# V in blocks of two tiles by seven half-size products instead of eight, spread over three slots, in a gated cross-attention and feed-forward kernel

## The chip, the cores and the metric

The kernel runs on one core of a Trainium2 chip. The metric is the device time of one execution in microseconds (us), the median of the runs shown. Five engines work beside each other, each through its own instructions in order: PE (TensorE, matrix products), ACT (ScalarE), DVE (VectorE), POOL (GpSimd) and SP (SyncE, which issues most of the DMAs). They wait for each other through semaphores.

## The reference

x is 8 batches of 1024 rows of 512 numbers; the context has the same shape.

```python
# cross-attention, causal, one head of 512
q, k, v = layernorm(x) @ w_q, ctx @ w_k, ctx @ w_v
attn = softmax(where(causal, q @ k.T / sqrt(512), -inf))
x = x + tanh(g_xattn) * (attn @ v)
# feed-forward, width 2048; w1 and w2 rounded to -1, 0, 1 by the mean of their absolute values
h = gelu(layernorm(x) @ ternary(W1).T + b1)
x = x + tanh(g_ffn) * (h @ ternary(W2).T + b2)
```

## The kernel before

Every number that enters a product is split into two fp16 parts, an upper one (the rounded value) and a lower one (the rest); ACT makes the upper part, DVE the lower. A product is then three passes: upper by upper, lower by upper, upper by lower (`PASSES`).

The rows of x are 64 tiles of 128, 8 tiles to a batch. The attention part goes in 64 slots, one for each tile t; below, n is t modulo 8, the tile's place in its batch. In a slot PE does, in this order (`slot`, L1304): the scores of tile t against its first n+1 context tiles (L1319, 12 matmuls for each 512 columns or part of them); the query product of tile t+2 (`t_product`, L1281, 24 matmuls of 256 columns); V of context tile t+1 (`v_product`, L1300, 12 matmuls of 512 columns); and attn times V of tile t-1 (here PV, L1349, 3(n) matmuls of 512 columns, 24 where n is 0). Scores need nothing of PV, so PV of one tile runs while the softmax of the next goes on.

DVE's slot (L897 to L986) runs in program order, so a late instruction makes all behind it late: add the causal mask (L909), the row maximum (L911) and the exponent's bias (L915); the statistics of the layer norm of tile t+5; the lower part of the softmax weights (L929); of the query product (L873); the normalised rows (L850); a ternary step for a chunk of weights in some slots (L1091, L1093); the lower part of V (L880); the output row (L956, L959, L963, after PV); and, in some slots, the maximum of the next batch's context (L821) or the lower part of that context (L756). ACT's slot follows the same chain: exponential (L573), upper part of the weights (L578), of the query product (L588), of the rows (L596), of V (L601), of the next context (L563). POOL makes the reciprocal root (L446) and the lower part of the rows (L450).

Near the end, the first rows of the feed-forward part are prepared: normalised by DVE from `FIRST_Y` on, summed by POOL into the blocks that seven half-size products need (`y_sums`), split (`y_upper` on ACT, `y_lower` on POOL), turned by a DMA on SP (`turn_y`, L334), and used by PE's first unit (`unit_first`, L1203), which runs in slot 63. DVE adds and subtracts blocks of the first weight matrix (`weight_sums`, L1004). The feed-forward part then runs 64 units, each with seven half-size products and 32 matmuls of 512 columns; the change moves a few steps into its first three.

Of the kernel before, what the change touches and what calls it, by code (L numbers as in the profile page):

```python
# [18 lines left out]
def gated_block(nc, x, ctxT, g_xattn, g_ffn, wqT, wkT, wv, w1T, b1c, w2T, b2, out):  # L19
    B, _, DC, S = ctxT.shape  # L20
# [26 lines left out]
    with es:  # L47
# [47 lines left out]
        cmax = sb("cmax", [P, 2])  # L95
# [16 lines left out]
        x2_in = raw[:, :].rearrange("p (t d) -> p t d", d=D)  # L112
# [17 lines left out]
        wS = [half for t in (a_s, wv_s)  # L130
# [10 lines left out]
        a_ps = y_ps = [s_ps[:, 0:D], s_ps[:, D:2 * D], e_ps[:, 0:D], e_ps[:, D:2 * D]]  # L141
        bank_a, bank_b, bank_c = [v_ps[:, :], o_ps[:, :]], m_ps[:, :], t_ps[:, :, :].rearrange("p a n -> p (a n)")
# [3 lines left out]
        ctx_in = sem("ctx_in")  # L146
        ctx_in0 = [sem(f"ctx_in0_{h}") for h in range(2)]
# [15 lines left out]
        turn_issued, turn_free = sem("turn_issued"), sem("turn_free")  # L163
        t_mm, t_hi, t_split = sem("t_mm"), sem("t_hi"), sem("t_split")
# [7 lines left out]
        w_loaded = [sem(f"w_loaded{i}") for i in range(WR)]  # L172
        w_summed, w_total, w_total_all, w_thresh = sem("w_summed"), sem("w_total"), sem("w_total_all"), sem("w_thresh")
# [12 lines left out]
        y_stored = [sem(f"y_stored{i}") for i in range(4)]  # L186
# [5 lines left out]
        def col(c, n=1):  # L192
# [7 lines left out]
        TOTALS = m_ps[:, 3 * P:3 * P + 2]  # L200
# [18 lines left out]

# [12 lines left out]

        PV0 = 2
# [13 lines left out]
        FIRST_Y = NT - 7  # L247
# [1182 lines left out]
```

## Time and profile before

| | |
|---|---|
| median of 3 runs (lowest, highest) | 1590.83 us (1590.52, 1591.98) |
| the profiled execution's own time | 1590.56 us |
| its span in the profile | 1588.7 us |
| matmuls, all passes | 10024 |
| granted TensorE clock, mean of the span | 0.997 of full speed |
| chain that ended last, by engine | PE 95%, DVE 3%, DMA 1%, issue 1% |

The span is what the profiler's records cover; 1.9 us of the execution lie around it. The attention part takes the first 756 us of the span, the feed-forward part the rest. One batch of eight slots takes 88.6 us on PE. The profile models the ends of matmuls, so the pace of PE is read from the starts of successive groups. In the timelines a row's start is when the instruction began on its engine, and two rows of one engine without a wait between them overlap by somewhat under 0.1 us.

### The profile page before, as it was taken

The page shows a single profiled execution, that of the slowest core. Times are in us where ns is not written, and L with a number is a line of the kernel's source. Part 1 is how long each engine was busy: PE and PEld are TensorE (multiplying, and loading weights), DVE is VectorE, ACT ScalarE, POOL GpSimd, SP SyncE. Part 2 cuts the span into 40 slices and gives each one's busy share as a digit, 9 for nine tenths or more (in the row PEclk, how much of TensorE's full clock was granted, in tenths as well). Part 3 has the DMA queues.
Part 4 walks back from the last instruction along what each step waited for, and adds up shares of the span by engine and source line. Part 5 has one row for each costly group of instructions (what it writes and reads, how often), then busy time and mean ns, then how long its engine had stood idle before and what let it go on. Part 6 is the DMA issues. An engine that isn't in the chain of part 4 may idle for free.

```text
span 1588.7 us, 26066 instructions
## 1 busy us (share of the span) xinstructions
PE 1567.5 (99%) x10024; PEld 979.6 (62%) x10024; DVE 1094.7 (69%) x1824; ACT 811.6 (51%) x1448; POOL 481.6 (30%) x468
## 2 busy tenths in 40 slices
PE   7899999999999999999999999999999999999998
PEld 4556555565656565564666666666666666666665
DVE  7766656577787777766567667766776676767654
ACT  2334444433332333333666666666666666666654
POOL 4311111111111111134144444444433453345330
PEclk9999999999999999999999999999999999999999
DMA  8547667654656655553322242233332332324110
GB/s 212 130 103 192 149 182 153 175 137 121 165 128 163 141 160 145 129 123 78 81 77 77 47 100 77 77 67 80 81 87 68 66 98 79 77 47 100 51 51 27
DMA packets 307964, 170.81 MB, mean 108 GB/s; under 512 B 268208, under 2 KB 268224, under 8 KB 306688
## 3 DMA queue, kind: packets, MB, share of 16 engines
q1 hardware_dynamic: 306368, 166.52, 43.0%
q10 hardware_dynamic: 1296, 2.36, 0.4%
q8 instruction: 79, 1.29, 0.3%
q14 instruction: 45, 0.37, 0.1%
q0 software_dynamic: 176, 0.27, 0.1%
HBM read 70.53 MB, written 33.55 MB: 66 GB/s over the span
## 4 chain that ended last, share of the span: by engine, by line
PE 95%; DVE 3%; DMA 1%; issue 1%; ACT 0%; SPq 0%; DVEq 0%
PE s_ps L1254 14%; PE e_ps L1254 14%; PE s_ps L1319 11%; PE o_ps L1349 11%; PE v_ps L1300 10%; PE t_ps L1281 10%; PE t_ps L1198 7%; PE o_ps L1198 7%; PE v_ps L1198 7%; PE m_ps L1198 3%; DMA ctx_s<-in_wqT 1%; DMA raw<-in_ctxT 0%; DVE cmax L821 0%; DVE wv_s L1004 0%; PE e_ps L1349 0%
## 5 line engine op out<-in xcount | busy, mean ns | idle before, releaser
L1056 DVE SCALAR_TENSOR_TENSOR v_s<-xnT,sc,v_s 128x512 f16<-128x512 f32 x256 | 239.0, 954 | 106.3 <-ACT v_s L681 106.3
L674 ACT ACTIVATE xnT<-tT,b_s 128x256 f32<-128x256 f32 x384 | 174.0, 500 | 182.9 <-DVE tT L1050 66.6
L1254 PE MATMUL s_ps<-w_s,v_s 128*128 128x512 f16 x1024 | 262.8, 379 | 0.0
L1254 PE MATMUL e_ps<-w_s,v_s 128*128 128x512 f16 x1024 | 262.8, 379 | 0.0
L573 ACT ACTIVATE p<-s_ps,ebias,esc 128x128 f32<-128x128 f32 (+3 forms) x64 | 53.2, 831 | 339.3 <-DVE ebias L915 339.3
L1319 PE MATMUL s_ps<-ctx_s,tT 128*128 128x512 f16 (+3 forms) x1152 | 197.7, 326 | 3.2 <-DVE tT L873 3.2
L1349 PE MATMUL o_ps<-v_s,pT 128*128 128x512 f16 x840 | 191.6, 379 | 0.1
L681 ACT ACTIVATE v_s<-xnT,sc 128x512 f16<-128x512 f32 x256 | 176.3, 712 | 7.5
L1300 PE MATMUL v_ps<-wv_s,ctx_s 128*128 128x512 f16 x768 | 176.5, 379 | 1.2 <-DVE v_s L880 0.8
L1254 PEld LDWEIGHTS e_ps<-w_s,v_s 128*128 128x128 f16 x1024 | 100.2, 98 | 120.8
L1281 PE MATMUL t_ps<-xnT,a_s 128*128 128x256 f16 x1488 | 172.7, 273 | 0.5 <-ACT a_s L649 0.5
L1319 PEld LDWEIGHTS s_ps<-ctx_s,tT 128*128 128x128 f16 x1152 | 105.8, 98 | 95.1 <-DVE tT L873 4.1
L1281 PEld LDWEIGHTS t_ps<-xnT,a_s 128*128 128x128 f16 x1488 | 144.8, 98 | 22.8 <-issue 0.9
L501 POOL TENSOR_TENSOR tT<-tT 128x512 f32<-128x512 f32 x64 | 81.5, 1273 | 245.7 <-ACT tT L701 245.7
L446 POOL TENSOR_TENSOR rstd<-var_s,minus_half 128x1 f32<-128x1 f32 x61 | 34.0, 557 | 382.8 <-DVE var_s L844 382.8
L1349 PEld LDWEIGHTS o_ps<-v_s,pT 128*128 128x128 f16 x840 | 82.1, 98 | 97.2 <-DMA pT<-p_s 0.6
L1254 PEld LDWEIGHTS s_ps<-w_s,v_s 128*128 128x128 f16 x1024 | 100.2, 98 | 67.1
L1300 PEld LDWEIGHTS v_ps<-wv_s,ctx_s 128*128 128x128 f16 x768 | 74.9, 98 | 78.9 <-issue 1.0
L450 POOL TENSOR_TENSOR xn_both<-xn_both 128x512 f16<-128x512 f32 x61 | 70.9, 1162 | 165.0 <-ACT xn_both L596 165.0
L1038 DVE COPY tT<-t_ps 128x512 f32<-128x512 f32 x64 | 44.3, 692 | 92.8 <-PE t_ps L1198 92.8
L471 POOL TENSOR_TENSOR rstd<-var_s,minus_half 128x1 f32<-128x1 f32 x64 | 35.1, 548 | 226.9 <-DVE var_s L1016 226.9
L880 DVE SCALAR_TENSOR_TENSOR v_s<-v_ps,v_s 128x512 f16<-128x512 f32 x64 | 44.1, 689 | 74.9 <-ACT v_s L601 74.9
(176 smaller groups left out, 2411.9 us busy)
## 6 DMA issues: line engine op xcount, KB each, us to landing
out_y<-x_ring SPq DMA_DIRECT2D x128, 256.0 KB, 2.2
x_ring<-in_x SPq DMA_DIRECT2D x63, 256.0 KB, 2.9
raw<-in_ctxT SPq DMA_DIRECT2D x7, 2048.0 KB, 7.9
raw<-out_y SPq DMA_DIRECT2D x44, 256.0 KB, 3.7
w_in<-in_w1T SPq DMA_DIRECT2D x16, 512.0 KB, 3.9
w_in<-in_w2T SPq DMA_DIRECT2D x16, 512.0 KB, 3.9
x_ring<-out_y SPq DMA_DIRECT2D x20, 256.0 KB, 3.5
xnT<-xn_both SPq DMA_TRANSPOSE x128, 2.7
```

What stands on the lines that cost most here:

```text
L450: g.tensor_tensor(xn_s[:, r, LO], xn32[:, r], xn_s[:, r, HI], ALU.subtract).then_inc(xn_lo, 1)
L501: g.tensor_tensor(rr[:, R3], rr[:, R3], rr[:, R5], ALU.add).then_inc(c22_sum, 1)
L573: a.activation(p32[:, 0:w], s_ps[:, 0:w], ACT.Exp, bias=ebias[:, r:r + 1], scale=esc[:, (s // TB) % 2:(s // TB) % 2 + 1], accum_out=rowsum ...
L674: a.activation(g32n[:, j, half * 2 * P:(half + 1) * 2 * P], src, ACT.Gelu, bias=b1_s[:, f:f + 1], scale=1.0 / YN).then_inc(g_act, 1)
L681: a.activation(g_s[:, U % 2, j, HI], g32n[:, j], ACT.Copy, scale=col(C_SG)).then_inc(g_hi, 1)
L1056: v.scalar_tensor_tensor(out=g_s[:, U % 2, j, LO], in0=g32n[:, j], scalar=col(C_SG), in1=g_s[:, U % 2, j, HI], op0=ALU.mult, op1=ALU.subtr ...
L1198: last_mm = mm(bank[:, p * 2 * P:(p + 1) * 2 * P], w, yT[g % 2][:, a, row, c, :], start=(first and p == 0 and a == HI and c == 0), stop=(a ...
L1254: last_mm = mm(y_ps[i], g_s[:, U % 2, j, a, i * P:(i + 1) * P], w2_s[:, f, :], start=(U % UG == 0 and n == 0 and a == HI), stop=(U % UG == ...
L1281: last_mm = mm(bank[:, dd], a_s[:, aa, c, d * P:(d + 1) * P], xnT[:, pr, xa, c, :], start=(n == 0 and c == 0), stop=(n == 2 and c == DC - 1))
L1300: last_mm = mm(v_ps[:, :], ctx_s[:, par, ca, c, j * P:(j + 1) * P], wv_s[:, va, c, :], start=(n == 0 and c == 0), stop=(n == 2 and c == DC ...
L1319: last_mm = mm(s_ps[:, lo:hi], tT[:, pr, ta, c, q * P:(q + 1) * P], ctx_s[:, par, ca, c, lo:hi], start=(n == 0 and c == 0), stop=(n == 2 a ...
L1349: last_mm = mm(o_bank(last, s), pT[:, (s - 1) % 2, pa, j], v_s[:, par, va, j], start=(n == 0 and j == 0), stop=(n == 2 and j == jn))
```

## The change

V of the first eight context tiles is made as before. The other 56 tiles are taken as 28 pairs of neighbouring tiles (u = 0 to 27). A pair's V is a 256 x 512 result from a 256 x 512 context block and the 512 x 512 weights; cut in halves each way it would be eight products of half size, and is made here by seven, of 6 matmuls of 256 columns each (three passes, two chunks). For this POOL makes four sums and differences of the context's blocks for each pair (`ctx_parts`), ACT and DVE split them (`ctx_parts_upper`, `ctx_parts_lower`), and the same is done once for the weights (slots 3 to 5). Products 1, 6, 5 and 3 add up in one PSUM region, and between them ACT copies the state out (`v_first`, `v_second`, `v_third`); product 2 has a region of its own, 7 and 4 share one. DVE adds three results (`v11`, `v22`, `v21`) and, with ACT, splits the four blocks of V (`v12_...`, `vd_...`, `v21_...`).

A pair's steps are spread over four slots: in slot 4+2u the context's sums and its split; in slot 5+2u products 1 and 2; in slot 6+2u product 6 right behind the scores, 5 and 7 behind the query product, 3 behind PV; in slot 7+2u product 4. So in a slot with even t PE does products 6, 5, 7, 3, and in one with odd t products 4, 1, 2 (4 of the pair before). Scales are lowered so that the sums fit into fp16.

With it go other moves. The context comes in quarters, each loaded, and its maximum taken, by itself in odd slots. The ternary step takes three instructions, in other slots, and its last three chunks move into the feed-forward part's first units. The feed-forward's second weight matrix lies where the context was loaded, and the rows of the first two groups are loaded one by one, a slot later (`FIRST_Y`); `weight_sums` come a slot earlier; the third `y_upper` and `y_lower` move into unit 0.

```diff
...
+        SPLIT_AT, PRE_AT, MAIN_AT, LAST_AT = 4, 5, 6, 7
...
+        def pair(t, at):
+            u, odd = divmod(t - at, 2)
+            return u if not odd and 0 <= u < NP else None
...
+        for b in range(2, B):
+            for q, at in enumerate((-3, -1, 1, 3)):
+                MAX_AT[TB * (b - 1) + at] = (b, (q,))
...
-                  **{b * TB + n: "T" for b in range(3, 7) for n in (4, 5, 6, 8)}}
+                  **{t: "T" for t in (29, 30, 31, 37, 38, 39, 45, 46, 53, 54, 55, 56, 60)}}
...
-        FIRST_Y = NT - 7
+        FIRST_Y = NT - 6
...
+            def ctx_parts(u):
...
+                pool.wait_ge(ctx_in[q], ctx_landed(b, q))
+                pool.wait_ge(sums_split, u)
+                g.tensor_tensor(sums32[:, 0], a21, a22, ALU.add).then_inc(sums_made, 1)
+                g.tensor_tensor(sums32[:, 2], a11, a21, ALU.subtract).then_inc(sums_made, 1)
+                pool.wait_ge(sums_made, 4 * u + 1)
+                g.tensor_tensor(sums32[:, 1], sums32[:, 0], a11, ALU.subtract).then_inc(sums_made, 1)
+                pool.wait_ge(sums_made, 4 * u + 3)
+                g.tensor_tensor(sums32[:, 3], a12, sums32[:, 1], ALU.subtract).then_inc(sums_made, 1)
...
+            def ctx_parts_upper(u):
+                act.wait_ge(sums_made, 4 * u + 4)
...
+            def v_third(u):
+                act.wait_ge(vp_mm[5], u + 1)
+                a.activation(vr[:, 1], vp_a, ACT.Copy).then_inc(vr_out, 1)
+            def v12_upper(u):
+                _, q, par = pair_at(u)
+                act.wait_ge(vp_mm[3], u + 1)
+                a.activation(v_s[:, par, HI, 2 * q, D // 2:D], vp_a, ACT.Copy, scale=V_DOWN).then_inc(vb_hi, 1)
...
+                if pre is not None:
+                    ctx_parts_upper(pre)
+                if main is not None:
+                    v_second(main)
                 if not last or t < NT:
                     softmax(it, s)
                 if not last or t < NT - T_LEAD:
...
+                if t + 1 < TB:
                     v_upper(it, s)
+                if main is not None:
+                    v_third(main)
+                if pre is not None:
+                    v_first(pre)
+                if tail is not None:
+                    v21_upper(tail)
+                if main is not None:
+                    v12_upper(main)
+                    vd_upper(main)
+                if split is not None:
+                    b, q, par = pair_at(split)
+                    ctx_upper(b, par, q)
...
+            def v22(u):
+                dve.wait_ge(vp_mm[7], u + 1)
+                dve.wait_ge(vr_out, nth_of(u, 3))
+                v.tensor_tensor(vr[:, 1], vr[:, 1], vp_c, ALU.add).then_inc(vb_sum, 1)
...
+            def v12_lower(u):
+                _, q, par = pair_at(u)
+                dve.wait_ge(vb_hi, nth_of(u, B12_DONE))
...
-                for m, n in terns[:1]:
-                    ternary(m, n)
-                if not last or t + 1 < NT:
+                if pre is not None:
+                    ctx_parts_lower(pre)
+                if tail is not None:
+                    v21(tail)
+                if pre is not None:
+                    v11(pre)
+                if tail is not None:
+                    v21_lower(tail)
+                if main is not None:
+                    v22(main)
...
+                if t + 1 < TB:
                     v_lower(it, s)
...
-                if last and t == NT - 2:
+                if last and t == NT - 3:
                     weight_sums(0)
                     weight_sums(1)
-                if last and t == NT - 1:
+                if last and t == NT - 2:
                     weight_sums(2)
                     weight_sums(3)
...
+                if main is not None:
+                    v12_lower(main)
+                    vd_lower(main)
+                if t == 1:
+                    ctx_lower(0, 0, 3)
+                if t in MAX_AT:
+                    batch, quarters = MAX_AT[t]
+                    for q in quarters:
+                        ins = ctx_quarter(batch, q)
...
+                if split is not None:
+                    b, q, par = pair_at(split)
+                    ctx_lower(b, par, q)
...
+                v.tensor_scalar(w_neg[:, :], src, col(nth), None, ALU.is_lt).then_inc(w_negs, 1)
+                v.tensor_scalar(w_dst(n), src, col(th), None, ALU.is_gt).then_inc(w_negs, 1)
+                dve.wait_ge(w_negs, 2 * n + 2)
+                v.tensor_tensor(w_dst(n), w_dst(n), w_neg[:, :], ALU.subtract).then_inc(w_ternary, 1)
...
+                left, right, bank, first = {
+                    1: (block(0, 0), weight(0, 0), vp_a, True),
+                    6: (part(1), weight_part(1), vp_a, False),
+                    5: (part(0), weight_part(0), vp_a, False),
+                    3: (part(3), weight(1, 1), vp_a, False),
+                    2: (block(0, 1), weight(1, 0), vp_b if u else vp_b0, True),
+                    7: (part(2), weight_part(2), vp_c, True),
+                    4: (block(1, 1), weight_part(3), vp_c, False)}[k]
+                for n, (ca, va) in enumerate(PASSES):
+                    for c in range(2):
+                        last_mm = mm(bank, left(ca, c), right(va, c), start=(first and n == 0 and c == 0),
+                                     stop=(n == 2 and c == 1), skip_group_check=True)
+                last_mm.then_inc(vp_mm[k], 1)
...
+            def v_six(u):
+                pe.wait_ge(vr_out, nth_of(u, 1))
+                pe.wait_ge(sums_split, u + 1)
...
+            def v_three(u):
+                pe.wait_ge(vr_out, nth_of(u, 3))
+                v_part(u, 3)
...
+                if main is not None:
+                    v_six(main)
                 if s > 0 and (not last or t < NT - T_LEAD):
                     t_product(it, s)
...
+                if main is not None:
+                    v_five(main)
+                    v_seven(main)
+                if tail is not None:
+                    v_four(tail)
+                if pre is not None:
+                    v_pre(pre)
...
-                if not last or t + 1 < NT:
+                if t + 1 < TB:
                     v_product(it, s)
...
                     last_mm.then_inc(pv_mm, 1)
+                if main is not None:
+                    v_three(main)
...
```

PE, slots 33 and 34 (n = 1 and 2) before: s_ps are the scores, t_ps the query product, v_ps V, o_ps PV.

```order
L1319 MATMUL s_ps<-ctx_s,tT 128x256 x12
L1281 MATMUL t_ps<-xnT,a_s 128x256 x24
L1300 MATMUL v_ps<-wv_s,ctx_s 128x512 x12
L1349 MATMUL o_ps<-v_s,pT 128x512 x3
L1319 MATMUL s_ps<-ctx_s,tT 128x384 x12
L1281 MATMUL t_ps<-xnT,a_s 128x256 x24
L1300 MATMUL v_ps<-wv_s,ctx_s 128x512 x12
L1349 MATMUL o_ps<-v_s,pT 128x512 x6
```

The same two slots in the changed kernel, where e_ps and v_ps at L1568 are the products:

```order
L1667 MATMUL s_ps<-ctx_s,tT 128x256 x12
L1628 MATMUL t_ps<-xnT,a_s 128x256 x24
L1568 MATMUL e_ps<-v_work,ctx_s 128x256 x6
L1568 MATMUL e_ps<-wv_s,ctx_s 128x256 x6
L1568 MATMUL v_ps<-wv_s,ctx_s 128x256 x6
L1713 MATMUL o_ps<-v_s,pT 128x512 x3
L1667 MATMUL s_ps<-ctx_s,tT 128x384 x12
L1568 MATMUL e_ps<-v_work 128x256 x6
L1628 MATMUL t_ps<-xnT,a_s 128x256 x24
L1568 MATMUL e_ps<-v_work 128x256 x12
L1713 MATMUL o_ps<-v_s,pT 128x512 x6
L1568 MATMUL e_ps<-wv_s,v_work 128x256 x6
```

In slot 33 products 4, 1 and 2 stand where V stood; in slot 34 product 6 has moved ahead of the query product, 5 and 7 stand where V stood, and 3 has come behind PV.

DVE, from the end of slot 32 (n = 0) into slot 33 before: L963 is the output row, L909 the next slot's mask.

```order
L880 SCALAR_TENSOR_TENSOR v_s<-v_ps,v_s 128x512
L956 RECIPROCAL rinv<-rowsum 128x1
L959 TENSOR_SCALAR osc<-rinv,fsc 128x1
L963 SCALAR_TENSOR_TENSOR x_ring<-o_ps,osc,x_ring 128x512
L909 TENSOR_TENSOR s_ps<-s_ps,causal 128x128
```

The same place in the changed kernel (L1047 is `v22`, L1059 `v12_lower`, L1067 `vd_lower`, L946 the lower part of the next context, L1164 the mask):

```order
L1047 TENSOR_TENSOR vr<-vr,e_ps 128x256
L1221 RECIPROCAL rinv<-rowsum 128x1
L1224 TENSOR_SCALAR osc<-rinv,fsc 128x1
L1228 SCALAR_TENSOR_TENSOR x_ring<-o_ps,osc,x_ring 128x512
L1059 SCALAR_TENSOR_TENSOR v_s<-e_ps,v_s 128x256
L1067 SCALAR_TENSOR_TENSOR v_s<-vr,v_s 128x2x256
L946 SCALAR_TENSOR_TENSOR ctx_s<-raw,csc,ctx_s 128x4x256
L1164 TENSOR_TENSOR s_ps<-s_ps,causal 128x128
```

Three instructions have come between the output row and the next slot's mask, where there was none; the first of them needs product 3 of the slot.

DVE, the second half of slot 33 before, up to the mask of slot 34 (L850 the normalised rows, L821 half of the context's maximum):

```order
L850 TENSOR_SCALAR xn_both<-x_ring,mv,rstd 128x512
L880 SCALAR_TENSOR_TENSOR v_s<-v_ps,v_s 128x512
L956 RECIPROCAL rinv<-rowsum 128x1
L959 TENSOR_SCALAR osc<-rinv,fsc 128x1
L963 SCALAR_TENSOR_TENSOR x_ring<-o_ps,osc,x_ring 128x512
L821 TENSOR_REDUCE cmax<-raw 128x1
L909 TENSOR_TENSOR s_ps<-s_ps,causal 128x128
```

And in the changed kernel (L1032 is `ctx_parts_lower`, L1053 `v21`, L1041 `v11`, L1075 `v21_lower`, L1017 a quarter of the maximum):

```order
L1104 TENSOR_SCALAR xn_both<-x_ring,mv,rstd 128x512
L1032 SCALAR_TENSOR_TENSOR v_work<-v_work,csc 128x1024
L1053 TENSOR_TENSOR vr<-vr,e_ps 128x256
L1041 TENSOR_TENSOR vr<-vr,v_ps 128x256
L1075 SCALAR_TENSOR_TENSOR v_s<-vr,v_s 128x256
L1221 RECIPROCAL rinv<-rowsum 128x1
L1224 TENSOR_SCALAR osc<-rinv,fsc 128x1
L1228 SCALAR_TENSOR_TENSOR x_ring<-o_ps,osc,x_ring 128x512
L1017 TENSOR_REDUCE cmax<-raw 128x1
L1164 TENSOR_TENSOR s_ps<-s_ps,causal 128x128
```

One instruction for V has become four, and the maximum is half as long.

## Rows read from the trace of the kernel before

**Rows 1.** which engine is busy, from the page (busy us, share, instructions)
```profile
PE 1567.5 (99%) x10024; PEld 979.6 (62%) x10024; DVE 1094.7 (69%) x1824; ACT 811.6 (51%) x1448; POOL 481.6 (30%) x468
```

**Rows 2.** PE's waits over the whole run (total us, times, longest us)
```profile
PE t_ps L1198 <- DVE wv_s L1004: 3.9, 1, 3.9
```

**Rows 3.** the timeline of PE, slots 25 and 26 (start us, length us, instructions)
```profile
311.32 5.34 PE L1349 MATMUL o_ps<-v_s,pT 128*128 128x512 f16 x24
316.50 1.47 PE L1319 MATMUL s_ps<-ctx_s,tT 128*128 128x256 f16 x12
317.81 2.78 PE L1281 MATMUL t_ps<-xnT,a_s 128*128 128x256 f16 x24
320.43 2.75 PE L1300 MATMUL v_ps<-wv_s,ctx_s 128*128 128x512 f16 x12
323.02 0.81 PE L1349 MATMUL o_ps<-v_s,pT 128*128 128x512 f16 x3
```

**Rows 4.** the timeline of DVE in the same slots
```profile
318.01 0.30 DVE L909 TENSOR_TENSOR s_ps<-s_ps,causal 128x128 f32<-128x128 f32 x1 [0.48 <-PE s_ps L1319]
...
320.19 0.43 DVE L929 SCALAR_TENSOR_TENSOR p_s<-p,p_s 128x256 f16<-128x256 f32 x1 [0.16 <-ACT p_s L578]
...
324.45 0.15 DVE L956 RECIPROCAL rinv<-rowsum 128x1 f32<-128x1 f32 x1
...
325.56 2.28 DVE L821 TENSOR_REDUCE cmax<-raw 128x1 f32<-128x2048 f32 x1
...
327.82 0.29 DVE L909 TENSOR_TENSOR s_ps<-s_ps,causal 128x128 f32<-128x128 f32 x1
...
330.34 0.56 DVE L929 SCALAR_TENSOR_TENSOR p_s<-p,p_s 128x384 f16<-128x384 f32 x1 [0.38 <-ACT p_s L578]
330.82 0.69 DVE L873 SCALAR_TENSOR_TENSOR tT<-t_ps,tT 128x512 f16<-128x512 f32 x1
331.43 0.54 DVE L850 TENSOR_SCALAR xn_both<-x_ring,mv,rstd 128x512 f32<-128x512 f32 x1
```

**Rows 5.** the timeline of ACT in the same slots
```profile
323.22 0.60 ACT L601 ACTIVATE v_s<-v_ps 128x512 f16<-128x512 f32 x1 [0.15 <-PE v_ps L1300]
...
332.54 0.58 ACT L601 ACTIVATE v_s<-v_ps 128x512 f16<-128x512 f32 x1
```

**Rows 6.** instructions by line and form (busy us, mean ns | idle before)
```profile
L756 DVE SCALAR_TENSOR_TENSOR ctx_s<-raw,csc,ctx_s 128x1024 f16<-128x1024 f32 x32 | 40.3, 1277 | 0.0
...
L563 ACT ACTIVATE ctx_s<-raw,csc 128x1024 f16<-128x1024 f32 x32 | 35.5, 1133 | 4.0 <-DVE csc L836 4.0
...
L641 ACT ACTIVATE v_s<-v_s 128x1792 f16<-128x1792 f32 x17 | 28.8, 1696 | 27.7 <-POOL v_s L482 27.7
...
L478 POOL TENSOR_TENSOR v_s<-v_s 128x256 f32<-128x256 f32 x17 | 12.3, 721 | 0.0
...
L1091 DVE TENSOR_SCALAR g<-w_in,sc 128x1024 f16<-128x1024 f32 x16 | 12.0, 748 | 0.1
...
L929 DVE SCALAR_TENSOR_TENSOR p_s<-p,p_s 128x256 f16<-128x256 f32 x8 | 3.4, 424 | 1.0 <-ACT p_s L578 1.0
L578 ACT ACTIVATE p_s<-p 128x256 f16<-128x256 f32 x8 | 3.3, 416 | 0.3
...
L1004 DVE TENSOR_TENSOR a_s<-a_s,w_s 128x1024 f16<-128x1024 f16 x2 | 1.3, 684 | 0.0
```

**Rows 7.** DVE while Pool works, a threshold instruction in slot 36
```profile
440.09 2.28 DVE L1093 SCALAR_TENSOR_TENSOR w_s<-w_in,sc,g 128x1024 f16<-128x1024 f32 x1
```

**Rows 8.** the timeline of POOL at the same time
```profile
440.13 1.16 POOL L450 TENSOR_TENSOR xn_both<-xn_both 128x512 f16<-128x512 f32 x1 [2.80 <-ACT xn_both L596]
```

**Rows 9.** the SP queue near the end of the attention part
```profile
722.68 4.24 SPq L334 DMA_TRANSPOSE ctx_s<-v_s  x1
```

**Rows 10.** the timeline of POOL just before that
```profile
719.07 3.59 POOL L488 TENSOR_TENSOR v_s<-v_s 128x1792 f16<-128x1792 f32 x1 [4.29 <-ACT v_s L641]
```

**Rows 11.** PE where the feed-forward part begins
```profile
736.04 1.04 PE L1198 MATMUL v_ps<-ctx_s,w_s 128*128 128x256 f16 x8
```

More of the change, by code:

```diff
@@ L19, in gated_block @@
 def gated_block(nc, x, ctxT, g_xattn, g_ffn, wqT, wkT, wv, w1T, b1c, w2T, b2, out):
-    B, _, DC, S = ctxT.shape
+    B, _, NQ, DC, QS = ctxT.shape
+    S = NQ * QS
     N, D = x.shape
@@ L129, in gated_block @@
         w1v = w1_s[:, :].rearrange("p (d c) (m b n) -> p d c m b n", d=2, c=2, m=FC // 2, b=2)
-        wS = [half for t in (a_s, wv_s)
+        wS = [half for t in (wv_s, a_s)
               for half in (t[:, 0].rearrange("p c d -> p (c d)"), t[:, 1].rearrange("p c d -> p (c d)"))]
@@ L185, in gated_block @@
         y_mm, y_done = sem("y_mm"), sem("y_done")
-        y_stored = [sem(f"y_stored{i}") for i in range(4)]
+        y_stored, X2_ALL = x2_stored[0:4], 16 * (NT // 8 + 1)
         (C_TANH0, C_TANH1, C_G0, C_G1, C_WMAX, C_BMAX, C_MA, C_PA, C_PW, C_PG, C_SA, C_SW, C_SG,
@@ L369, in slot @@
                 if t == 1:
-                    load_ctx(1)
-                if s % TB == 7 and (not last or t + 9 < NT):
-                    load_ctx(it * 2 + s // TB + 2)
+                    for q in range(NQ):
+                        load_ctx(1, q)
             for i in range(8):
                 sp.sem_inc(x2_stored[i], 16)
-            for i in range(4):
-                sp.sem_inc(y_stored[i], 16)
             for r in range(2):
@@ L460, in slot @@
                         y_sums(e // 2)
[L461 removed]
+                if last and e in (2, 4):
                     y_lower(e // 2 - 1)
@@ L538, in _ @@
                     last_sum(U + 1)
+                if U == 0:
+                    y_lower(2)
                 if U in ROWS_Q0:
@@ L723, in _ @@
                     unit_copy(U + 1)
+                if U == 0:
+                    y_upper(2)
                 if U - 1 in ROWS_Q0:
@@ L900, in slot @@
                 i, r = s % TB, s % 2
+                split, pre, main, tail = pair(t, SPLIT_AT), pair(t, PRE_AT), pair(t, MAIN_AT), pair(t, LAST_AT)
                 terns = w_turn(t, "T")
@@ L1247, in back @@
                 pe.wait_ge(g_split, 4 * U + n + 1)
+                if U < UG and n == 0:
+                    pe.wait_ge(w_ternary, NW // 2 + 2 * U + 2)
                 for i in range(GT):
@@ L1306, in slot @@
                 i = s % TB
+                pre, main, tail = pair(t, PRE_AT), pair(t, MAIN_AT), pair(t, LAST_AT)
                 if not last or t < NT:
```

348 lines of the change are left out of this document (262 added, 86 removed).

## The prediction

> **What bounds the kernel now.** I read the busy shares first, then PE's waits, then the timelines of slots 25 and 26 (n = 1 and 2, where slots are shortest). PE is busy for 99% of the span and DVE for 69% [rows 1]; the largest wait of PE outside the start is one of 3.9 us [rows 2]. So PE's work is the time, and work taken from PE is time saved, as long as PE is not made to wait. The reader should see in the timelines how little protects that. DVE is late already: the scores of slot 26 follow PV at 323.02 + 0.65, take 1.95 and so end near 325.6, but the mask comes at 327.82, behind the context's maximum [rows 3, 4]. That costs nothing before, since PE uses a slot's softmax only in the next slot.
>
> **PE's work.** 24 matmuls of 512 columns take 316.50 - 311.32 = 5.18 us, 24 of 256 take 320.43 - 317.81 = 2.62, V of one tile 323.02 - 320.43 = 2.59 [rows 3]. A pair cost 5.18; seven products are 42 matmuls of 256, 42 x 2.62/24 = 4.585. The difference of 0.595 by 28 pairs is **-16.7 us**. Accumulating into a region read in between changes nothing in this pace; each such read is a wait, taken below.
>
> A rule speaks against this. The Trainium skill (TensorE: Matmul & The Clock Gate, section Back-to-back issue gap) gives a sustained spacing of about 131 ns for 512 columns and 81 ns for 128; an estimate between them is 98 ns for 256, and by it a pair would rise from 3.1 to 4.1 us, +27 us in all. The rows show 216 and 109 ns in this kernel; the measurement decides.
>
> **The new wait, n = 2.** Product 3 of an even slot waits for `v_third`, which ACT reaches only behind softmax, query product and normalised rows of the same slot, and these hang on DVE. PE now needs DVE's slot within the slot. I follow it from E, the end of product 3 in the slot n = 0.
> - ACT starts 0.20 after PE's end (323.02 to 323.22) [rows 3, 5]. `v12_upper` 0.42, `vd_upper` 0.60, the context's upper part 1.13, then its lower part on DVE 1.28 [rows 5, 6]; less some 0.25 of overlap, DVE is free for the mask of n = 1 at E + 3.4. The scores are there at E + 1.5 (316.50 to 318.01) [rows 3, 4]: 1.9 late.
> - Slot n = 1 on DVE: mask to softmax's lower part 2.18, to the query product's 0.48, to the normalised rows 0.61 [rows 4], these 0.46; `ctx_parts_lower` 1.20 (as the context's, 1.28 less overlap) [rows 6]; `v21`, ACT's `v21_upper` and gaps 0.91; `v21_lower` 0.36 (all three 256 wide, 0.42 each) [rows 6], held 0.3 by POOL (below); reciprocal to maximum 1.11, a quarter maximum half of 2.28, 1.14 [rows 4]. Sum 8.75: mask of n = 2 at E + 12.15.
> - Slot n = 2: 2.52 + 0.48 + 0.61 [rows 4], to ACT's instruction behind the rows 1.11 (331.43 to 332.54) [rows 4, 5], `v_third` 0.42, start of PE 0.1: product 3 can start at E + 17.4.
> - PE is there at: slot 1, 1.31 + 2.62 + 18 x 0.109 + 0.65 = 6.54; slot 2, 1.95 + 0.65 + 2.62 + 1.31 + 1.29 = 7.82; E + 14.4. **Wait 3.0 us.**
>
> No row shows a 256-wide sum from PSUM: 128 wide is 0.30, 512 wide 0.69 [rows 4], so the five 256-wide links give -0.65 to +1.35; I take 0.42, from rows of that width. The wait is then 2.1 (without POOL) to 4.4. It comes in slots 10, 18, 26, 34, 42 and 50: **+18.0**. In slot 58 no maximum stands before it (-1.14), but statistics of a feed-forward row do (+0.8): **+2.65**. At n = 1 nothing on PE waits, since the next scores need only the exponential, ready near E + 5.2.
>
> **POOL.** In slot 36 a DVE instruction of 1024 with two inputs in SBUF took 2.28 us while POOL's 1.16 us ran, against 1.28 for one of that shape alone [rows 6 to 8]: one waits for the other's end. The change adds four POOL instructions of 0.72 [rows 6] per pair, right behind the normalised rows of the odd slot, where DVE's ternary steps now also stand. The Trainium skill (SBUF — State Buffer, section Who interferes with whom) says that a DVE instruction with two SBUF inputs, or in a two-port mode, and a POOL instruction reading SBUF exclude each other for a whole instruction; by that rule the upper ends below hold, and the trace agrees in slot 36.
> - n = 6 after a ternary step in slot 29, 37, 45 or 53: the step is 2 x 0.75 + 0.68 [rows 6], some 2.1 with overlap. Same chain from the slot n = 4, with PV of 18 matmuls as cover: product 3 waits 0.65 if POOL does not interfere, 2.9 if it takes turns with each of the three. I take the middle, 1.8, three times, and 0.9 for slot 54 (no maximum before it; 0 to 1.8): **+6.3**.
> - n = 0 after a step in slot 31 or 39: PV has 24 matmuls of cover; 0 to 1.1, I take 0.5 twice: **+1.0**.
> - n = 4 without a step: the chain comes out 0 to 0.6 behind PE; 0.3 six times: **+1.8**.
> The step itself was 0.75 + 2.28 [rows 6, 7]; that it gets shorter saves nothing on PE.
>
> **The end of the attention part.** Before, the second block of rows was turned from 722.68 to 726.92 [rows 9], and PE's first unit began at 736.04 [rows 11], 9.1 later. Now the rows are made a slot later, and slots 61 and 62 are shorter by a V each. From the start of the scores of slot 62: scores 12 x 896 columns 4.53, PV of 18 3.89, scores of slot 63 5.18, so PE wants the first unit at 13.6 [rows 3]. Mask at 4.7; softmax's lower part 3.9 behind it (2.52 at 384 columns, 0.34 more per 128 [rows 4]); about then ACT starts `y_upper`, 1.70 [rows 6], to 10.3; POOL's `y_lower` 3.59 [rows 10], to 13.9; the turn 4.24 [rows 9], to 18.1. That is a wait of 4.6. If `weight_sums` and POOL exclude each other, the output row of slot 62 comes near 17, SP stands at its store before the turn, and the wait is 8.1. I take 6.4. In exchange `weight_sums` come a slot earlier, and the 3.9 us wait for them [rows 2] goes: **+2.5** (0.7 to 4.2).
>
> **The rest.** In the first units `y_upper`, `y_lower` and three ternary chunks are added. PE is covered by the units' own products; the longest of them, 3.59 [rows 10], bounds the cost; I take **+0.8** (0 to 3.6). The context's quarters carry the same bytes as before and land some 7 us ahead of their maximum. They are issued before the turn of the softmax weights on SP, which then still has 2 us until PV. I cost this, and the sums for the weights in slots 3 to 5 (V as before is still in these slots, so they are 11 us and more), at 0; without that cover each would cost up to 2.
>
> **Sum.** -16.7 + 18.0 + 2.65 + 6.3 + 1.0 + 1.8 + 2.5 + 0.8 = +16.4 on the profiled execution's 1590.56 (span 1588.7 and 1.9 around it; 0.27 under the median of the runs): **1607.0 us**.
>
> **Rivals.**
> - *POOL and DVE hardly meet* (POOL runs its sums before DVE gets to its own). For it: POOL is 30% busy and starts at once when the rows are ready. Against it: slot 36. Then n = 2 is 6 x 2.7 + 2.35, n = 6 3 x 0.65, the rest of the locks 0, the end and the units as above: -16.7 + 18.55 + 1.95 + 3.3 = +7.1, 1597.7.
> - *DVE keeps up, faster than before.* If the chain from E to product 3 took 14.4 instead of 17.4, only the end and the units would be left: -16.7 + 3.3 = -13.4, 1577.2; with one us of wait per batch 1584. It decides from 16.0 down: there 7 x 1.6 + 3.3 = 14.5 against 16.7 is about nothing. For it: DVE is 69% busy, and PE waited for it hardly at all. Against it: the order in DVE's queue, which the change lengthens on both sides of the shortest slot.
> - *The gain is eaten just so* (chain 15.5 to 16.2, at most one of the smaller waits): 1587.6 to 1594.
> - *Worse*: every 256-wide link at its upper end and POOL in the way of each step: over 1618.
> - That 256 columns cost more than half of 512, as the Trainium skill's figures would have it (1618 by the +27), gets no chance of its own, since both widths run here. That the products do not run as written is excluded by the order of the instructions.
>
> **How the numbers follow.** Forecast (1600 to 1618) 0.48; POOL aside (1594 to 1600) 0.20; over 1618 0.07; eaten 0.10; faster 0.15. What a measurement can tell from no change is 0.2%, 3.2 us, so below 1587.6 is faster, and to 1594.0 the same: faster 0.15, same 0.10, slower 0.75. The range that holds the time 8 times in 10 runs from 1586 to 1618: it leaves out 0.07 above and most of the faster case below. The forecast's own range is 1600 to 1618.
>
> **What would show it.** PE's busy time falls by some 17 us, and PE's list of waits gets a new first line: product 3 waiting for ACT's `v_third`, 15 to 30 us in total, about 3 us in slots 10, 18, 26, 34, 42, 50, 58, less in others. DVE's mask in slots n = 1 comes about 3.4 us after product 3 of the slot before. A batch of eight slots takes more than the 86.2 us of its matmuls (88.6 less four pairs by 0.595), near 89. PE waits 5 to 8 us at the first unit for the turned rows. A list of waits with under 7 us for product 3 proves the main step wrong, and ternary steps of 2.2 us beside POOL the turns with it.

## The result: slower by 1.7%, and the profile after

The changed kernel takes 1617.9 us (median of four runs, 1615.8 to 1620.9) against 1591.4 on the same chip: a ratio of 1.0169 with a 95% interval of 1.0156 to 1.0183, +26.5 us. The forecast was 1607.0, its range 1586 to 1618. The sign was right, the size too small by 11 us. The profiled execution took 1617.88 us, its span is 1616.1.

First the busy shares of the kernel after, which answer to [rows 1].

```profile
PE 1564.6 (97%) x10528; PEld 1029.7 (64%) x10528; DVE 1171.2 (72%) x1996; ACT 877.8 (54%) x1589; POOL 591.9 (37%) x585
```

PE was idle for 1616.1 - 1564.6 = 51.5 us, before for 1588.7 - 1567.5 = 21.2: **30.3 us more waiting**. The prediction's waits add up to 33. But PE's busy time fell by 2.9 us only, where 16.7 were forecast. That is where the account is out.

The waits of PE after (total us, times, longest us), which answer to [rows 2]:

```profile
PE e_ps L1568 <- ACT vr L719: 18.9, 10, 2.2
PE v_ps L1472 <- issue: 10.7, 1, 10.7
PE s_ps L1667 <- DVE tT L1127: 4.1, 3, 1.9
...
PE e_ps L1568 <- DVE ctx_s L946: 1.7, 1, 1.7
...
PE v_ps L1472 <- ACT tT L885: 1.0, 1, 1.0
```

The first line is product 3 waiting for `v_third`, the second the first unit waiting for the turned rows (put down to "issue", since nothing but a DMA came last). The 3.9 us for the weight sums are gone. The fourth line is product 1 of the very first pair, in slot 5.

The timelines of PE, DVE and ACT in slot 18 (n = 2), which answer to [rows 3 to 5]; each line has start and length in us, and in brackets the idle time before it and what ended it:

```profile
245.94 1.47 PE L1568 MATMUL e_ps<-v_work 128*128 128x256 f16 x12
247.25 1.46 PE L1713 MATMUL o_ps<-v_s,pT 128*128 128x512 f16 x6
250.88 0.83 PE L1568 MATMUL e_ps<-wv_s,v_work 128*128 128x256 f16 x6 [2.18 <-ACT vr L719]
251.55 2.75 PE L1667 MATMUL s_ps<-ctx_s,tT 128*128 128x512 f16 x12
```

```profile
245.75 0.29 DVE L1164 TENSOR_TENSOR s_ps<-s_ps,causal 128x128 f32<-128x128 f32 x1
...
249.35 0.54 DVE L1104 TENSOR_SCALAR xn_both<-x_ring,mv,rstd 128x512 f32<-128x512 f32 x1
```

```profile
248.13 0.58 ACT L762 ACTIVATE tT<-t_ps 128x512 f16<-128x512 f32 x1
249.93 0.63 ACT L770 ACTIVATE xn_both<-xn_both 128x512 f16<-128x512 f32 x1 [1.21 <-DVE xn_both L1104]
250.46 0.37 ACT L719 ACTIVATE vr<-e_ps 128x256 f32<-128x256 f32 x1
```

Products 5 and 7 are done at 247.25, PV at 248.71. But ACT stands idle for 1.21 us until DVE's rows are there, and reads the bank out behind them: PE waits 2.18 us. This is the predicted mechanism. Twelve products of 256 columns take 247.25 - 245.94 = 1.31 us, the pace that the forecast used.

**What the forecast did not have** shows in slot 34, where the wait is as long as in slot 18. PE's timeline there, and then the windows (each line has the stretch and its length in us, PE's busy us with its instructions, the granted clock as a share of full speed, the busy share of the DMA engines, GB/s):

```profile
430.69 1.46 PE L1568 MATMUL e_ps<-wv_s,v_work 128*128 128x256 f16 x6 [2.18 <-ACT vr L719]
431.94 3.79 PE L1667 MATMUL s_ps<-ctx_s,tT 128*128 128x512 f16 x12
```

```profile
426.00:428.00 2.00, 2.00 (x17) 1.00 0.58 124
428.00:430.00 2.00, 0.51 (x3) 1.00 0.55 155
430.00:432.00 2.00, 1.31 (x7) 0.66 0.48 101
432.00:434.00 2.00, 2.00 (x6) 0.50 0.37 132
434.00:436.00 2.00, 2.00 (x12) 0.99 0.63 129
```

Behind the wait the granted clock stands at 0.50, the lower of its two levels (1.2 GHz), for some 3 us. The same twelve scores that take 2.75 us in slot 18 take 3.79, and product 3 before them 1.46, not 0.83. That is 1.6 us on top of the wait. In slot 18 nothing of the kind follows: it happens behind some of the waits. In this execution it follows four of the six waits of 2.1 to 2.2 us (slots 10, 34, 42 and 50). In all, from slot 8 on PE is busy for 19.25 us at the lower level: 13.59 behind these four waits and 5.66 where the feed-forward part begins.

The kernel before shows the same once, behind its 3.9 us wait for the weight sums [rows 2], where eight matmuls take 1.89 us and not 1.04 as in [rows 11]:

```profile
748.13 1.89 PE L1198 MATMUL t_ps<-ctx_s,wv_s 128*128 128x256 f16 x8 [3.89 <-DVE wv_s L1004]
```

The end of the attention part, which answers to [rows 9 to 11]: DVE, POOL, the SP queue and PE in turn.

```profile
732.49 0.55 DVE L1296 TENSOR_SCALAR v_s<-x_ring,mv,rstd 128x512 f32<-128x512 f32 x1 [4.63 <-POOL v_s L607]
...
749.31 5.74 DVE L1270 TENSOR_TENSOR a_s<-w_s,wv_s 128x1024 f16<-128x1024 f16 x2
...
755.40 0.75 DVE L1228 SCALAR_TENSOR_TENSOR x_ring<-o_ps,osc,x_ring 128x512 f32<-128x512 f32 x1
```

```profile
748.73 4.10 POOL L607 TENSOR_TENSOR v_s<-v_s 128x1792 f16<-128x1792 f32 x1 [1.97 <-ACT v_s L831]
```

```profile
756.18 0.34 SPq L453 DMA_DIRECT2D out_y<-x_ring  x1
756.57 4.48 SPq L410 DMA_TRANSPOSE ctx_s<-v_s  x1
```

```profile
738.12 4.71 PE L1667 MATMUL s_ps<-ctx_s,tT 128*128 128x512 f16 x24 [1.52 <-DVE tT L1127]
...
762.89 1.86 PE L1472 MATMUL v_ps<-ctx_s,w_s 128*128 128x256 f16 x8 [10.70 <-issue]
764.55 1.91 PE L1472 MATMUL t_ps<-ctx_s,wv_s 128*128 128x256 f16 x8
```

POOL's `y_lower` was done at 752.83, but the turn of its rows went out at 756.57: SP stood at a store that waits for DVE's output row, and this stood behind two weight sums stretched beside `y_lower` and POOL's next instruction (5.74 us for both; two others, at 739.22, took 1.29). From the end of the turn in SP's queue, 761.05, to PE's start pass another 1.84. And behind the wait the first eight matmuls show 1.86 us where they showed 1.04 before [rows 11]: the lower clock again.

### The profile page after: what moved, and what is told of

Same layout as the page of the kernel before. It is cut to its first block, busy times and chain, and to the rows that moved or that the text cites. A ratio compares the mean times of both kernels' runs of the same rounds, so it can differ in the third digit from the quotient of the medians.

```text
span 1616.1 us, 27825 instructions
## 1 busy us (share of the span) xinstructions
PE 1564.6 (97%) x10528; PEld 1029.7 (64%) x10528; DVE 1171.2 (72%) x1996; ACT 877.8 (54%) x1589; POOL 591.9 (37%) x585
## 4 chain that ended last, share of the span: by engine, by line
PE 76%; DVE 13%; ACT 5%; issue 4%; POOL 1%; DMA 0%; DVEq 0%; SPq 0%; ACTq 0%
PE s_ps L1530 13%; PE e_ps L1530 13%; PE o_ps L1713 7%; PE s_ps L1667 7%; PE t_ps L1472 7%; PE v_ps L1472 7%; PE o_ps L1472 7%; PE t_ps L1628 5%; PE e_ps L1568 5%; PE m_ps L1472 3%; DVE negmax L1166 1%; DVE ctx_s L946 1%; DVE xn_both L1104 1%; DVE cmax L1017 1%; ACT p_s L752 1%
## 5 line engine op out<-in xcount | busy, mean ns | idle before, releaser
L1530 PE MATMUL s_ps<-raw,v_s 128*128 128x512 f16 x1024 | 262.8, 379 | 0.8 <-DVE raw L1366 0.8
L1530 PE MATMUL e_ps<-raw,v_s 128*128 128x512 f16 x1024 | 262.8, 379 | 0.0
L1667 PE MATMUL s_ps<-ctx_s,tT 128*128 128x512 f16 (+3 forms) x1152 | 205.0, 333 | 4.5 <-DVE tT L1127 4.1
L1530 PEld LDWEIGHTS e_ps<-raw,v_s 128*128 128x128 f16 x1024 | 100.2, 98 | 120.8
L1530 PEld LDWEIGHTS s_ps<-raw,v_s 128*128 128x128 f16 x1024 | 100.1, 98 | 68.1 <-issue 1.1
L539 POOL TENSOR_TENSOR xn_both<-xn_both 128x512 f16<-128x512 f32 x61 | 79.1, 1296 | 161.5 <-ACT xn_both L770 161.5
L770 ACT ACTIVATE xn_both<-xn_both 128x512 f16<-128x512 f32 x64 | 40.4, 631 | 94.0 <-DVE xn_both L1104 91.1
L1316 DVE TENSOR_TENSOR tT<-tT,t_ps 128x512 f32<-128x512 f32 x64 | 44.1, 688 | 51.2 <-ACT tT L885 28.1
L1184 DVE SCALAR_TENSOR_TENSOR p_s<-p,p_s 128x128 f16<-128x128 f32 (+3 forms) x64 | 48.6, 759 | 43.9 <-ACT p_s L752 43.9
```

Source lines behind the costliest of these rows:

```text
L539: g.tensor_tensor(xn_s[:, r, LO], xn32[:, r], xn_s[:, r, HI], ALU.subtract).then_inc(xn_lo, 1)
L1530: last_mm = mm(y_ps[i], g_s[:, U % 2, j, a, i * P:(i + 1) * P], w2_s[:, f, :], start=(U % UG == 0 and n == 0 and a == HI), stop=(U % UG == ...
L1667: last_mm = mm(s_ps[:, lo:hi], tT[:, pr, ta, c, q * P:(q + 1) * P], ctx_s[:, par, ca, c, lo:hi], start=(n == 0 and c == 0), stop=(n == 2 a ...
```

## The experiments

All are edits of the changed kernel, except where a run builds on another, and all were run beside the kernel before. Its median lies between 1590.9 and 1591.4 us on each of the chips, so the times below are compared across them.

**1. The read-out for product 3 earlier on ACT.**

```diff
+                if main is not None:
+                    v_third(main)
                 if not last or t + LN_LEAD < NT:
                     rows_upper(it, s)
 ...
-                if main is not None:
-                    v_third(main)
                 if pre is not None:
```

> ACT reads out the bank for product 3 (v_third) right behind its half of the query product, no longer behind the normalised rows, which DVE makes late; nothing else is changed. Theory (ACT's order makes product 3 wait): in slot 18 the query product's upper part ends at 248.71, the read-out takes 0.37, so product 3 waits some 0.45 us instead of 2.18. The line 'product 3 waits for v_third' falls from 18.9 us to 2 to 5, the four drops of the clock behind these waits (about 1.7 us each) go, and the time falls by 14 to 24 us, to 1594 to 1604. Rival (DVE is short of time in the slots n = 0 to 2, whoever reads the bank): the wait comes back as a wait of the scores for DVE's half of the query product, or stays at product 3, together over 12 us, and the time stays above 1609.

Measured: 1595.1 us (1594.3 to 1597.0), ratio 1.0025 (1.0015 to 1.0034): 22.8 us less from two moved lines. The line in PE's waits, and slot 18 on PE and ACT:

```profile
PE e_ps L1568 <- ACT vr L719: 2.0, 6, 0.3
```

```profile
247.61 0.83 PE L1568 MATMUL e_ps<-wv_s,v_work 128*128 128x256 f16 x6 [0.34 <-ACT vr L719]
```

```profile
247.18 0.38 ACT L719 ACTIVATE vr<-e_ps 128x256 f32<-128x256 f32 x1
248.50 0.63 ACT L770 ACTIVATE xn_both<-xn_both 128x512 f16<-128x512 f32 x1 [0.94 <-DVE xn_both L1104]
```

The theory holds: it was ACT's order, not DVE's load. The waits fell by 16.9 us and the time by 22.8, so some 6 us more went with them; in the profiles PE's busy time fell by 8.3 us (1564.6 to 1556.3). The end (10.8 us there) is as before the edit.

**2. Matmuls in the waits of slots n = 2.**

```diff
+                if t % TB == 2 and main is not None:
+                    for _ in range(20):
+                        mm(m_ps[:, 2 * P:4 * P], a_s[:, HI, 0, 0:P], a_s[:, HI, 1, 0:2 * P], start=True, stop=True)
                 if main is not None:
                     v_three(main)
```

> The changed kernel with 20 matmuls of 256 columns (2.18 us at 0.109) on PE ahead of product 3 in the slots n = 2, into columns of a bank that nobody reads there: the wait stays as long, but PE is busy in it. It shows the price of the waits through the clock alone. Theory (a wait of about 2 us can halve the clock of the matmuls behind it, 1.7 us each time, four times in the profiled run): the line of product 3 falls to 4 to 7 us, PE's busy time grows by some 15 less 7, no stretch behind these slots shows a clock of 0.5 to 0.9, and the time falls by 5 to 9 us, to 1609 to 1613. Rival (only the length of the waits costs, and the clock's drops are part of the wait or of the records): the time stays within 2 us of 1617.9.

Measured: 1612.8 us (1611.9 to 1617.2), 5.1 less than the changed kernel's 1617.9, with a wide scatter. The line of product 3 fell to 4.3 us. In its profile no slot behind a filled wait shows a lowered clock. PE does more work, the edit makes no other engine earlier, and the kernel is faster.

**3. Two weight sums behind the output row.**

```diff
-                if last and t == NT - 2:
-                    weight_sums(2)
-                    weight_sums(3)
 ...
+                if last and t == NT - 2:
+                    weight_sums(2)
+                    weight_sums(3)
                 if main is not None:
                     v12_lower(main)
```

> weight_sums(2) and (3) in slot 62 stand behind the output row on DVE, no longer ahead of it; nothing else is changed. Theory (the weight sums that shared time with POOL held the output row, SP stood at that row's store, and the turn of the second block of rows, ready at 752.8, was issued at 756.6): the store is out by 751, the turn follows y_lower's end, and PE's wait at the first unit falls from 10.7 to some 7 us (6 to 8); the time falls by 3 to 4.5 us, to 1613.5 to 1615. Rival (the wait's length comes from the rows themselves, from POOL's y_lower and the turn with its landing): the wait stays above 9.5 us and the time within 1.5 us of 1617.9.

Measured: 1610.8 us (1610.3 to 1613.1), 7.1 less, more than either theory gave. POOL, SP and PE at the end:

```profile
747.48 3.58 POOL L607 TENSOR_TENSOR v_s<-v_s 128x1792 f16<-128x1792 f32 x1 [1.96 <-ACT v_s L831]
```

```profile
751.08 4.25 SPq L410 DMA_TRANSPOSE ctx_s<-v_s  x1
```

```profile
757.23 1.86 PE L1472 MATMUL v_ps<-ctx_s,w_s 128*128 128x256 f16 x8 [6.29 <-issue]
```

The turn now goes out 0.02 us behind `y_lower`, and the wait falls by 4.4 us. The rest of the 7.1 need not be this edit's: PE's busy time is 4.0 us less too (1560.6 for 1564.6), and in this execution the clock fell behind two of the six waits of 2.2 us (slots 10 and 50) and not behind four. Run 7 tests that.

**4. A first rearrangement of the end, which missed.** `y_upper(0)` on ACT ahead of `v12_upper`, `y_upper(1)` ahead of the softmax, all weight sums behind the feed-forward rows:

```diff
+                if last and t == FIRST_Y + 4:
+                    y_upper(1)
                 if not last or t < NT:
                     softmax(it, s)
 ...
+                if last and t == FIRST_Y + 2:
+                    y_upper(0)
                 if pre is not None:
                     v_first(pre)
```

> Only the end of the attention part is rearranged: y_upper(0) on ACT in slot 60 ahead of v12_upper, y_upper(1) in slot 62 ahead of the softmax, and the four weight sums on DVE behind the output row and the normalised feed-forward row of slots 61 and 62. Theory (late y_upper and early weight sums make the end slow: DVE stood 4.6 us for y_lower(0), the scores of slot 62 1.5 us, PE 10.7 us at the first unit, at half clock for some 5 us behind it): DVE's idle time ahead of slot 61's mask goes, the wait at the first unit falls to 0 to 4 us and the clock stays up: the time falls by 9 to 13 us, to 1605 to 1609. Rival (a new wait for the weight sums takes its place, as the 3.9 us of the kernel before): 4 us or more at the first or second unit's products, time 1611 or more.

Measured: 1613.7 us (1611.2 to 1616.7): the theory missed. The scores of slot 62 wait no more, but the first unit still waits 8.6 us. The time and this wait lie where the rival had them, but its cause, the weight sums, is not the one. DVE, then POOL:

```profile
723.93 3.96 DVE L1368 TENSOR_TENSOR raw<-raw,g 128x1024 f16<-128x1024 f16 x1
...
746.61 3.31 DVE L1186 SCALAR_TENSOR_TENSOR p_s<-p,p_s 128x896 f16<-128x896 f32 x1 [1.81 <-ACT p_s L752]
```

```profile
723.54 3.80 POOL L607 TENSOR_TENSOR v_s<-v_s 128x1792 f16<-128x1792 f32 x1 [2.94 <-ACT v_s L833]
...
745.39 3.58 POOL L607 TENSOR_TENSOR v_s<-v_s 128x1792 f16<-128x1792 f32 x1
```

Both DVE instructions with two inputs in SBUF that met a `y_lower` here were held until it was over, and end 0.55 and 0.95 us behind it: 3.96 us instead of 0.69, 3.31 instead of 1.09. At the second `y_lower` it was the softmax's lower part of slot 62, whose turn and store stand ahead of the second turn on SP.

**5. The end arranged by who waits, on top of run 1.** The main edits (besides, `y_upper(1)` as in run 4, all weight sums behind the output row of slot 62, and PE's second step waiting for two more of them):

```diff
-                if last and t in (FIRST_Y + 3, FIRST_Y + 5):
-                    turn_y((t - FIRST_Y - 3) // 2)
+                if last and t in (FIRST_Y + 3, FIRST_Y + 4):
+                    turn_y(t - FIRST_Y - 3)
 ...
-                if last and e in (2, 4):
-                    y_lower(e // 2 - 1)
+                if last and e in (2, 3):
+                    y_lower(e - 2)
 ...
+                if y_row == 3:
+                    y_normal(2)
                 if norm:
                     ln_rows(k, rk, src, s + LN_LEAD >= 2)
 ...
                     v21_lower(tail)
+                if y_row == 3:
+                    y_normal(3)
```

> v_third early on ACT (as in the run with that alone), and the end of the attention part arranged by who waits: DVE's normalised feed-forward rows 2 and 3 stand in slot 61 behind its half of the query product and behind v21_lower, all four weight sums behind the output row of slot 62; POOL's y_lower(1) stands in slot 61, ACT's y_upper(1) ahead of the softmax of slot 62, the second turn ahead of that slot's turn of the softmax on SP; PE's second step waits for two more sums. Theory (the chain normalised rows, POOL's sums, y_upper, y_lower, turn, 1.9 us to PE's start, sets the 10.8 us wait, not a lack of time on any engine): the scores of slot 62 wait no more (1.5 us), the first unit waits 0 to 3 us, the half clock behind it goes (1.5 to 2.5): 1595.1 less 10 to 14 is 1581 to 1585. Rival (DVE and POOL exclude each other over the 3.6 us of y_lower, and the wait returns at the weight sums or at the softmax of slot 62, as in the first rearranged end): first or second unit waits over 5 us, time 1588 or more.

Measured: 1585.4 us (1584.4 to 1587.3), ratio 0.9963 (0.9951 to 0.9976): 9.7 less than run 1, a little under the 10 to 14 of the theory. The first unit's wait for the turned rows is gone, 1.2 us for weight sums and 1.6 for a turned softmax came.

**6. Also products 1 and 2 of the first pair behind V of slot 5.**

```diff
-                if pre is not None:
+                if pre:
                     v_pre(pre)
 ...
                     v_product(it, s)
+                if pre == 0:
+                    v_pre(pre)
```

> As the run before it, and PE's products 1 and 2 of the very first pair (slot 5) stand behind V of that slot, no longer ahead of it. Theory (product 1 waits 1.7 to 2.1 us there for DVE's half of the context's first quarter, and V covers 2.6 us): that line of the waits goes, and the time falls by 1 to 3.5 us against the run before, to 1579 to 1583. Rival (the read-out of product 1 then comes too late for product 6 in slot 6): a wait of 1 to 2 us at product 6, the time the same within 1 us.

Measured: **1581.9 us** (1581.4 to 1583.6), ratio 0.9938 (0.9925 to 0.9952), 3.5 less than run 5: the wait (2.1 us there) is gone and none took its place. Not all of the 3.5 need be this edit's, since the clock fell once at 743.6 us in run 5's profile and not in run 6's. This version beats both kernels. Its PE where the feed-forward part begins:

```profile
728.87 1.03 PE L1475 MATMUL v_ps<-ctx_s,w_s 128*128 128x256 f16 x8 [0.93 <-DMA ctx_s<-v_s]
729.74 1.04 PE L1475 MATMUL t_ps<-ctx_s,wv_s 128*128 128x256 f16 x8
```

**7. Runs 1 and 3 together.** The diffs of runs 1 and 3, word for word.

> The two single edits together: v_third early, and weight sums 2 and 3 behind the output row of slot 62. Theory (both causes are independent, and of the 7.1 us of the second edit alone some 4.4 are its wait and the rest came from the clock behind other waits): 1595.1 less 4 to 6, 1589 to 1591.5. Rival (the second edit's 7.1 us are all its own): 1587 to 1588.5.

Measured: 1591.5 us (1589.2 to 1594.1), 3.6 less than run 1, a little under the 4 to 6 of the theory and far from the rival. So the edit of run 3 is worth about its wait. The other 3 us there go with the clock behind other waits: in run 8's profile, of the unedited kernel, the clock falls behind one such wait, and it is only 4.9 us above run 3's (1615.9 and 1611.0).

**8 and 9. The changed kernel again, and with the long waits of product 3 and the first unit filled.** The filling stands ahead of `v_three` and of the first unit:

```diff
+            def fill(n):
+                for _ in range(n):
+                    mm(m_ps[:, 2 * P:4 * P], v_s[:, 1, HI, 0, 0:P], v_s[:, 1, HI, 0, 0:2 * P], start=True, stop=True)
 ...
+                if last and t == NT - 1:
+                    fill(90)
 ...
+                if main is not None:
+                    fill(20 if t % TB == 2 else 10 if t in (30, 38, 46) else 0)
```

> The changed kernel itself once more, beside the filled one on the same chip: 1616 to 1620.

> The changed kernel with matmuls of 256 columns on PE in every long wait of the attention part: 20 ahead of product 3 in the slots n = 2, 10 (1.1 us) in slots 30, 38 and 46, 90 (9.8 us) ahead of the first unit; into columns that nobody reads there. All waits keep their length for the other engines. Theory (a wait of PE has a second price beside its length, the slower clock of the matmuls behind it): no stretch from slot 8 to the first units shows a clock under 0.9, the three products of the first unit take 0.9 us each and not 1.7, and the time is 6 to 11 us under the changed kernel's own of the same chip. Rival (the matmuls behind a wait are slower because of what ended the wait, reads of freshly written buffers or DMA traffic, or the drops are chance): the products of the first unit stay at 1.7 us, and the time within 3 us of the changed kernel's.

Measured on one chip: 1617.6 us (1615.9 to 1618.8) for the changed kernel, 1611.9 (1610.4 to 1614.0) filled: 5.7 us less, the ranges apart, a little under the 6 to 11 expected. PE in slot 34 and at the first unit, filled:

```profile
428.16 2.35 PE L1539 MATMUL m_ps<-v_s 128*128 128x256 f16 x20
430.50 0.83 PE L1573 MATMUL e_ps<-wv_s,v_work 128*128 128x256 f16 x6
431.16 2.75 PE L1672 MATMUL s_ps<-ctx_s,tT 128*128 128x512 f16 x12
```

```profile
747.25 9.99 PE L1539 MATMUL m_ps<-v_s 128*128 128x256 f16 x90
758.18 1.03 PE L1472 MATMUL v_ps<-ctx_s,w_s 128*128 128x256 f16 x8 [0.95 <-issue]
759.05 1.04 PE L1472 MATMUL t_ps<-ctx_s,wv_s 128*128 128x256 f16 x8
```

With PE busy through the wait, the same work behind it runs at 0.87 us per eight and 2.75 for the scores. From slot 8 on the granted clock is 1.00 throughout. What slows the matmuls is PE's idling, not the data that ends the wait.

## Why the prediction was right in its sign and wrong in its size

**The step that failed is "PE's work: -16.7 us"**, read as time: it took for granted that the matmuls keep their pace whatever PE waits, and so priced each wait by its length alone. The work did fall: a pair costs 42 matmuls at the predicted 0.109. But of the 11 us by which the profiled execution passes the sum, -2.7 is in the waits and +13.8 in PE's busy time; of the prediction's own signs, busy time down by some 17 us failed. Of these 13.8, 9.4 go with the waits: the same 10528 matmuls keep PE busy for 1564.6 us here and 1555.2 in run 6, which has no long waits of product 3 or the first unit. Two things show that they are the clock. The 19.25 us of work at half pace from slot 8 on, of which run 6 has none, cost 9.6. And most of it lies in matmuls that the change does not touch, the scores (before, after, run 6; busy us, mean ns | idle before):

```profile
L1319 PE MATMUL s_ps<-ctx_s,tT 128*128 128x512 f16 (+3 forms) x1152 | 197.7, 326 | 3.2 <-DVE tT L873 3.2
```

```profile
L1667 PE MATMUL s_ps<-ctx_s,tT 128*128 128x512 f16 (+3 forms) x1152 | 205.0, 333 | 4.5 <-DVE tT L1127 4.1
```

```profile
L1672 PE MATMUL s_ps<-ctx_s,tT 128*128 128x512 f16 (+3 forms) x1152 | 197.8, 326 | 3.4 <-DVE tT L1129 2.2
```

The other 4.4 are also in run 6. They are not in V and its products, which take 16.5 us less there than V before, counted from start to start. Where they come from stays open; a part may be the ends of groups ahead of a wait, since PV's six matmuls in slot 18 count as busy for 1.46 us, and six at 0.216 take 1.30.

That the waits as a whole came within 2.7 us of the sum is luck in part. Product 3 was forecast 10.9 us too high (29.75 with all its terms, 18.9 measured), and the end 6.4, the first units 1.7 and slot 5 1.7 too low. That the time fell just inside the range is luck too: no rival had a slower clock behind a wait, and the one over 1618 was built on longer waits.

The filled waits show 5.1 and 5.7 us of the clock's price in the medians, and run 1 some 6 that went with its waits. The Trainium skill (TensorE: Matmul & The Clock Gate, section HAM oscillation — how this bites in real kernels) describes a kernel in which each wait for data sends TensorE back to its slow clock, so that this is paid again every time. The trace agrees in part: of 24 unfilled waits of 2.1 to 2.2 us in four profiles (the changed kernel twice, runs 3 and 4), 8 were followed by the low clock; of 12 filled ones (runs 2 and 9) none. What decides which waits are followed by it, no run shows.

Term by term, against the forecast:

- *Product 3, n = 2*: six times 3.0 forecast, 2.18 (once 2.11) measured; slot 58 1.57, not 2.65. Counted from the end of product 3 in slot 16 (233.85), product 3 of slot 18 began after 17.0 us (17.4 forecast), and PE was there after 14.9 (14.4): half of the difference is the chain's, half PE's. The 0.3 for POOL did not arise; POOL was the one held, its instruction for the rows in slot 17 taking 1.47 us and not the 1.16 of slot 18. DVE's mask of slot 17 came at 237.29, 3.44 behind that end (3.4 forecast).
- *n = 6 after a ternary step*: 6.3 forecast, 4.3 measured (1.90, 1.22, 1.22). The turns beside POOL are real: in slot 29 DVE's three instructions (first fence) met POOL's sums (second):

```profile
374.95 1.27 DVE L1363 TENSOR_SCALAR g<-w_in,sc 128x1024 f16<-128x1024 f32 x1
376.14 1.21 DVE L1364 TENSOR_SCALAR w_s<-w_in,sc 128x1024 f16<-128x1024 f32 x1
377.38 1.10 DVE L1366 TENSOR_TENSOR w_s<-w_s,g 128x1024 f16<-128x1024 f16 x1
```

```profile
375.63 1.17 POOL L563 TENSOR_TENSOR v_work<-v_work,raw 128x256 f32<-128x256 f32 x1
```

  3.45 us until DVE's next instruction, against 2.1 alone. Without a step (n = 4), and at n = 0, PE waited not at all; +2.8 were forecast.
- *The end*: +2.5 forecast; the first unit's wait grew by 6.8, to 10.7 against an upper bound of 8.1, and the scores of slots 58 and 62 gained 2.1 more. Three things were missing in the wait and behind it. The upper case ("SP stands at its store") had no landing time of the turn, 1.8 to 2.1 us in all these runs. Rows 2 wait on DVE for `y_lower(0)`, since both blocks share a buffer, and this put the mask of slot 61 back by some 3 us. And the slow clock behind the wait.
- *First units*: +0.8 forecast, 2.5 measured (1.02, 0.82 and 0.65). *Slots 3 to 5*: 0 with "up to 2" without cover, 1.7 measured in slot 5.

The lock between DVE and POOL, which the prediction weighed with the Trainium skill (SBUF — State Buffer, section Who interferes with whom), cost some 1.3 us at a ternary step in the slots (3.45 for 2.1) and more at the end, where POOL's instruction is 3.6 us long: run 4 shows 3.31 for 1.09. The rule says that the two exclude each other for a whole instruction; the trace of run 4 agrees.

## What to carry to other kernels

A wait on TensorE has two prices, its length and the slower clock that may follow; the second shows as busy time, so compare the busy time of unchanged matmuls, and test it by filling the wait with dummy matmuls. When a consumer moves into the slot of its producer, look at the order of the engine that reads the result out: what it does there should not stand behind an instruction that waits for a third engine, and here two moved lines were worth 22.8 us. Before a long POOL instruction is placed, list which DVE instructions with two SBUF inputs can meet it, and who stands in a queue behind them.

## What was not expected of the hardware

- Waits of the same 2.18 us are sometimes followed by half the clock and sometimes not, within one execution (slots 18 and 34). Four runs of the changed kernel lie between 1615.8 and 1620.9, the kernel before between 1590.5 and 1592.1. That this scatter comes from it is not shown run by run; the fastest of the four had a mean granted clock of 0.991, the other three 0.988.
- Filling PE's idle time with useless matmuls made the kernel 5.1 (run 2) and 5.7 us (run 9) faster.
- From the end of a row turn in the SP queue to the matmul that needs it pass 1.84 us in the changed kernel, 1.90 in run 3 and 2.07 in run 6.
